# Layer-0 cross attention: weights normalised by token ahead of their transposes, outputs made feature by token, queries' bias on ScalarE

## The reference, cut to what matters

```python
g = jax.nn.relu(jnp.einsum('bnmd,hd->bhnm', emb, Wg) + bg[None, :, None, None])
q = (queries @ Wq.T + bq).reshape(b, nq, H, D_K).transpose(0, 2, 1, 3)
k = (keys @ Wk.T + bk).reshape(b, nk, H, D_K).transpose(0, 2, 1, 3)
v = (values @ Wv.T + bv).reshape(b, nk, H, D_V).transpose(0, 2, 1, 3)
a = jnp.einsum('bhqd,bhkd->bhqk', q, k) / jnp.sqrt(jnp.float32(D_K))
mn = jax.nn.softmax(jnp.log(jnp.clip(g, 1e-06, None)) + a, axis=-1)
out = jnp.einsum('bhqk,bhkd->bqhd', mn, v).reshape(b, nq, H * D_V)
return out @ Wo.T + bo
```

## Time and profile before

| what | value |
|---|---|
| median of three runs | 413.66 us (411.83 to 413.72) |
| the profiled execution, its own time | 412.39 us |
| its span in the trace | 410.6 us |
| mean granted TensorE clock | 0.91 of full speed |
| busy: TensorE, weight loads, DVE, ACT, GpSimd | 81%, 48%, 70%, 49%, 22% of the span |

### The profile page before, as it was taken

The page is one execution under the profiler, slowest core; times in us unless marked ns, Lnnn a source line. Parts: engine busy times, 40 slices in busy tenths (PEclk is TensorE's granted clock), DMA queues, the critical chain, the costliest instruction groups (busy, mean ns, idle before and its releaser), DMA issues.

```text
span 410.6 us, 8844 instructions
## 1 busy us (share of the span) xinstructions
PE 333.1 (81%) x3743; PEld 196.8 (48%) x3743; DVE 285.9 (70%) x420; ACT 201.5 (49%) x329; POOL 89.4 (22%) x85
## 2 busy tenths in 40 slices
PE   5277899999986999999998869647769986899721
PEld 1022333333322678889886634212247773577610
DVE  2779587888998666777766336898458746667475
ACT  2986976788986423222233435843424424243330
POOL 4101353455663270000000000000043412122000
PEclk9765899999999999999999999967989999699955
DMA  6920000023735500000000000000000000000001
GB/s 177 395 105 0 1 1 2 0 69 93 202 101 153 204 3 2 2 3 2 3 2 3 0 2 1 0 0 0 0 2 3 3 3 3 2 3 3 2 2 51
DMA packets 22137, 16.42 MB, mean 40 GB/s; under 512 B 17873, under 2 KB 19153, under 8 KB 21970
## 3 DMA queue, kind: packets, MB, share of 16 engines
q1 hardware_dynamic: 22098, 15.86, 12.1%
HBM read 11.13 MB, written 4.72 MB: 39 GB/s over the span
## 4 chain that ended last, share of the span: by engine, by line
PE 60%; DVE 18%; ACT 14%; issue 6%; DMA 1%; POOL 0%; DVEq 0%; SPq 0%; ACTq 0%; POOLq 0%
PE psum L441 52%; PE psum L754 3%; PE psum L623 2%; DVE small L1553 2%; PE psum L590 2%; ACT arena_b L996 1%; DVE arena_b L1415 1%; ACT psum L992 1%; DVE small L1629 1%; ACT arena_b L976 1%; ACT psum L987 1%; ACT logg L939 1%; ACT arena_b L982 1%; ACT arena_b L1134 1%; DVE arena_b L1599 1%
## 5 line engine op out<-in xcount | busy, mean ns | idle before, releaser
L441 PE MATMUL psum<-arena_b 64*64 64x9 f32 (+2 forms) x1316 | 46.2, 258 | 8.7 <-DVE arena_b L1633 5.5
L1227 POOL TENSOR_TENSOR arena_a<-arena_a,arena_b 128x1024 f32<-128x1024 f32 x15 | 31.8, 2121 | 62.2 <-DVE arena_b L1389 62.2
L441 PEld LDWEIGHTS psum<-arena_b 64*64 64x64 f32 (+2 forms) x1316 | 26.9, 137 | 22.8 <-issue 16.1
L1401 DVE TENSOR_TENSOR_SCAN arena_a<-arena_b,psum 128x512 f32<-128x512 f32 x32 | 37.4, 1206 | 0.4
L441 PE MATMUL psum<-arena_a,xw 128*128 128x128 f32 x256 | 33.5, 286 | 2.2 <-ACT arena_a L1041 2.2
L441 PE MATMUL psum<-arena_a 64*64 64x64 f32 (+2 forms) x1088 | 34.0, 245 | 0.3 <-DVE xn L1317 0.3
L441 PEld LDWEIGHTS psum<-arena_a,xw 128*128 128x128 f32 x256 | 31.2, 199 | 3.7 <-ACT arena_a L1041 2.7
L1629 DVE TENSOR_REDUCE small<-psum 128x16 f32<-128x1024 f32 x16 | 19.6, 1224 | 19.0 <-PE psum L441 19.0
L441 PEld LDWEIGHTS psum<-arena_a 64*64 64x64 f32 (+1 forms) x1088 | 21.8, 138 | 18.6 <-issue 9.6
L1262 POOL MEMSET arena_b<- 128x16 f32 x4 | 0.3, 128 | 139.3 <-DVE x L1619 139.3
L441 PE MATMUL psum<-xc,logg 128*128 128x512 f32 x32 | 21.3, 754 | 10.2 <-DVE sq L1375 10.2
(11 more groups left out here) (222 smaller groups left out, 671.6 us busy)
## 6 DMA issues: line engine op xcount, KB each, us to landing
g_scratch<-arena_a SPq DMA_DIRECT2D x64, 64.0 KB, 2.1
logg<-in_rkvo SPq DMA_DIRECT2D x8, 256.0 KB, 4.5
xw<-in_xw SPq DMA_DIRECT2D x1, 2048.0 KB, 10.7
logg<-g_scratch SPq DMA_DIRECT2D x2, 1024.0 KB, 5.1
logg<-g_scratch SPq DMA_DIRECT2D x1, 2048.0 KB, 7.8
ffn_w<-in_ffn SPq DMA_DIRECT2D x1, 576.0 KB, 11.3
x<-in_xT SPq DMA_DIRECT2D x2, 256.0 KB, 3.4
arena_a<-in_ctxT SPq DMA_DIRECT2D x1, 512.0 KB, 6.4
```

Source lines behind the costliest of these rows:

```text
L441: return nc.tensor.matmul(o, l, r, start=start, stop=stop, **kw)
L1227: g.tensor_tensor(two, two, pairs[n % 3][:, :, HALF + 1:], ALU.add).then_inc(s.ab_done, 1)
L1401: return v_.tensor_tensor_scan(sums[n % 3][:, i * HALF:(i + 1) * HALF], pairs[n % 3][:, i, 0:HALF], scan_mask, 0.0, ALU.add, ALU.mult)
```

## The change

Three things change in the cross attention, and with them the order on TensorE and ACT.

The softmax is finished before the transposes. The exponential is taken on the shifted scores in SBUF (ACT), then DVE sums them per token and head, takes the reciprocal and multiplies, and only then are the weights transposed; ACT copies the transposed weights. The values lose their column of ones, and GpSimd its four memsets.

The product is turned round. Values are now the stationary operand and weights the moving one, so that the outputs come as features by tokens, as the output projection wants them. The eight output transposes are gone, and ACT copies the outputs straight from pD.

The bias of the queries goes from two DVE operations to eight ACT operations with the bias as a column per partition. For the first tile they stand behind the second half of the layer norm on ACT.

TensorE's order for tile t is now: scores, keys t+1, product t-1, queries t+1, Wo t-1, values t+1, transposes t. The product's matmuls go over the sequence and the partition half within each pair of heads; before they went over both halves and then the next pair. Some semaphores are merged.

```diff
-OUT_HEADS = [4 * (i // 2) + 2 * par + i % 2
-             for par, i in [(0, i) for i in range(1, 8)] + [(1, i) for i in range(7)] + [(1, 7), (0, 0)]]
+OUT_HEADS = [4 * j + 2 * par + i for par in range(2) for j in range(4) for i in range(2)]
...
-            def x_out_transposed(t, u):
-                pe.wait_ge(s.on_done, t + 1)
-                for cc in range(NCH):
-                    last = nc.tensor.transpose(pB[:, cc * P:(cc + 1) * P], on_x[u][:, cc * P:(cc + 1) * P], ident)
-                last.then_inc(s.to_psum, 1)
+            def x_product(t, u):
+
+                pe.wait_ge(s.pt_done, t + 1)
+                pe.wait_ge(s.vx_done, 2 * t + 2)
+                if t:
+                    pe.wait_ge(s.x2_done, t)
+                for i in range(8):
+                    for b in range(2):
+                        for par in range(2):
+                            r = slice(64 * par, 64 * par + 64)
+                            at = P * (i // 2) + 64 * b
+                            last = mm(half(pD, par)[64 * (i % 2):64 * (i % 2) + 64, at:at + 64], v_x[u][b][r, i, :],
+                                      pt_x[u][r, 4 * (i % 2) + i // 2, 64 * b:64 * b + 64])
+                last.then_inc(s.o_psum, 1)
...
             def xattn(t, u, prev, nxt):
-                pe.wait_ge(s.q_done, 2 * t + 2)
+                pe.wait_ge(s.q_done, t + 1)
...
                 if prev:
-                    x_out_transposed(t - 1, 1 - u)
+                    x_product(t - 1, 1 - u)
+                pe.wait_ge(s.s_scaled, t + 1)
                 if nxt:
-                    pe.wait_ge(s.s_scaled, t + 1)
                     x_q(t + 1)
                 if prev:
                     x_wo(t - 1, 1 - u)
-                pe.wait_ge(s.s_done, t + 1)
-                if prev:
-                    pe.wait_ge(s.ot_done, t)
-                for cc in range(NCH):
-                    last = nc.tensor.transpose(pB[:, cc * P:(cc + 1) * P], s_x[u][:, cc * P:(cc + 1) * P], ident)
-                last.then_inc(s.t_psum, 1)
                 if nxt:
                     x_v(t + 1, 1 - u)
                 else:
...
-                pe.wait_ge(s.pt_done, t + 1)
-                pe.wait_ge(s.vx_done, 2 * t + 2)
+                pe.wait_ge(s.p_done, t + 1)
                 if prev:
-                    pe.wait_ge(s.x2_done, t)
-                for i in range(8):
-                    for par in range(2):
-                        for b in range(2):
-                            bank, at = o_place(par, i)
-                            r = slice(64 * par, 64 * par + 64)
-                            last = mm(bank[64 * b:64 * b + 64, at:at + 65],
-                                      pt_x[u][r, 4 * (i % 2) + i // 2, 64 * b:64 * b + 64], v_x[u][b][r, i, :])
-                last.then_inc(s.o_psum, 1)
+                    pe.wait_ge(s.pt_done, t)
+                for cc in range(NCH):
+                    last = nc.tensor.transpose(pB[:, cc * P:(cc + 1) * P], s_x[u][:, cc * P:(cc + 1) * P], ident)
+                last.then_inc(s.t_psum, 1)
...
-            x_out_transposed(TILES - 1, 1)
+            x_product(TILES - 1, 1)
             x_wo(TILES - 1, 1)
...
+            def x_queries(t, u):
+                act.wait_ge(s.q_psum, t + 1)
+                for cc in range(NCH):
+                    last = nc.scalar.activation(q_x[u][:, cc, :], pA[:, cc * P:(cc + 1) * P], ACT.Identity,
+                                                bias=p("xbq", cc))
+                last.then_inc(s.q_done, 1)
+
+            def x_exp(t, u):
+                act.wait_ge(s.s_done, t + 1)
+                nc.scalar.activation(s_x[u], s_x[u], ACT.Exp).then_inc(s.s_exp, 1)
+
+            def x_weights(t, u):
+                act.wait_ge(s.t_psum, t + 1)
+                nc.scalar.activation(pt_x[u].rearrange("p c t -> p (c t)"), pB[:, :], ACT.Copy).then_inc(s.pt_done, 1)
+
             def x_out(t, u):
-                act.wait_ge(s.to_psum, t + 1)
-                nc.scalar.activation(ot_x[u].rearrange("p c t -> p (c t)"), pB[:, :], ACT.Copy).then_inc(s.ot_done, 1)
+                act.wait_ge(s.o_psum, t + 1)
+                nc.scalar.activation(ot_x[u].rearrange("p c t -> p (c t)"), pD[:, :], ACT.Copy).then_inc(s.ot_done, 1)
 
             def xattn(t, u, prev, nxt):
                 if prev:
+                    x_weights(t - 1, 1 - u)
                     x_out(t - 1, 1 - u)
-                act.wait_ge(s.t_psum, t + 1)
-                nc.scalar.activation(pt_x[u].rearrange("p c t -> p (c t)"), pB[:, :], ACT.Exp).then_inc(s.pt_done, 1)
+                x_exp(t, u)
                 if nxt:
-                    if prev:
-                        act.wait_ge(s.o_psum, t)
+                    x_queries(t + 1, 1 - u)
                     x_values(t + 1, 1 - u)
...
             ln_rstd(1, 1)
-            act.wait_ge(s.v_ones, 4)
+            act.wait_ge(s.g_psum, 2 * BOX_STEPS)
+            x_queries(0, 0)
             x_values(0, 0)
...
             ln_square(2, 0)
+            x_weights(TILES - 1, 1)
             ln_rstd(2, 0)
...
             def xattn(t, u, prev, nxt):
-                if prev:
-                    x_norm(t - 1, 1 - u)
                 dve.wait_ge(s.s_psum, t + 1)
...
                 if nxt:
                     x_keys(t + 1, 1 - u)
-                if nxt:
-                    x_queries(t + 1, 1 - u)
+                total, inv = small[:, 64:80], small[:, 96:112]
+                dve.wait_ge(s.s_exp, t + 1)
+                v_.tensor_reduce(total, heads(s_x[u]), axis=AX.X, op=ALU.add).then_inc(s.s_sum, 1)
+                dve.wait_ge(s.s_sum, t + 1)
+                v_.reciprocal(inv, total).then_inc(s.s_inv, 1)
+                dve.wait_ge(s.s_inv, t + 1)
+                v_.tensor_tensor(heads(s_x[u]), heads(s_x[u]), cols(inv, S), ALU.mult).then_inc(s.p_done, 1)
                 if prev:
                     x_residual(t - 1)
...
-            x_queries(0, 0)
             ln_scale(1, 1)
```

More of the change, by code:

```diff
@@ L146, in build_program @@
         k_x = [ca(NCH * P).rearrange("p (c t) -> p c t", c=NCH) for _ in range(2)]
-        v_x = [[ca(8 * 65).rearrange("p (i d) -> p i d", i=8) for _ in range(2)] for _ in range(2)]
+        v_x = [[ca(8 * 64).rearrange("p (i d) -> p i d", i=8) for _ in range(2)] for _ in range(2)]
         q_x = [ca(NCH * P).rearrange("p (c t) -> p c t", c=NCH) for _ in range(2)]
@@ L150, in build_program @@
         pt_x = [ca(1024).rearrange("p (c t) -> p c t", c=NCH) for _ in range(2)]
-        on_x = [ca(1024) for _ in range(2)]
         ot_x = [ca(1024).rearrange("p (c t) -> p c t", c=NCH) for _ in range(2)]
@@ L273, in build_program @@
         s.o_psum = sem("o_psum")
-        s.o_inv = sem("o_inv")
-        s.on_done = sem("on_done")
-        s.to_psum = sem("to_psum")
+        s.s_exp = sem("s_exp")
+        s.s_sum = sem("s_sum")
+        s.s_inv = sem("s_inv")
+        s.p_done = sem("p_done")
         s.ot_done = sem("ot_done")
@@ L1239, in _ @@
                     r_y(n - 1)
-            pool.wait_ge(s.g_psum, 2 * BOX_STEPS)
-            for u in range(2):
-                for b in range(2):
-                    g.memset(v_x[u][b][:, :, 64:65], 1.0).then_inc(s.v_ones, 1)
             w3 = ffn_w[:].rearrange("p (k i) -> p k i", i=BLK)
@@ L1250, in _ @@
             pool.wait_ge(s.w_s, 1)
-            g.tensor_tensor(t3, w3, cols(wq_r, BLK), ALU.mult).then_inc(s.w_n, 1)
-            pool.wait_ge(s.w_n, 1)
-            g.tensor_scalar(wq_t, wq_t, MAGIC, MAGIC, ALU.add, ALU.subtract).then_inc(s.w_r, 1)
-            pool.wait_ge(s.w_r, 1)
-            g.tensor_scalar(wq_t, wq_t, 7.0, -8.0, ALU.min, ALU.max).then_inc(s.w_c, 1)
-            pool.wait_ge(s.w_c, 1)
+            g.tensor_tensor(t3, w3, cols(wq_r, BLK), ALU.mult).then_inc(s.w_step, 1)
+            pool.wait_ge(s.w_step, 1)
+            g.tensor_scalar(wq_t, wq_t, MAGIC, MAGIC, ALU.add, ALU.subtract).then_inc(s.w_step, 1)
+            pool.wait_ge(s.w_step, 2)
+            g.tensor_scalar(wq_t, wq_t, 7.0, -8.0, ALU.min, ALU.max).then_inc(s.w_step, 1)
+            pool.wait_ge(s.w_step, 3)
             g.tensor_tensor(t3, t3, cols(wq_s, BLK), ALU.mult).then_inc(s.w_q, 1)
@@ L1466, in _ @@
             residual1(1)
-            def x_queries(t, u):
-                dve.wait_ge(s.q_psum, t + 1)
-                for k in range(2):
-                    v_.tensor_tensor(q_x[u][:, 4 * k:4 * k + 4, :], half(pA, k).rearrange("p (c t) -> p c t", c=4),
-                                     cols(p("xbq")[:, 4 * k:4 * k + 4], P), ALU.add).then_inc(s.q_done, 1)
             def x_keys(t, u):
@@ L1478, in x_keys @@
                     .then_inc(s.kx_done, 1)
-            def x_norm(t, u):
-                dve.wait_ge(s.o_psum, t + 1)
-                inv = small[:, 64:80]
-                banks = [bank[:, :].rearrange("p (k c) -> p k c", k=2)[:, :, 0:65 * n]
-                         .rearrange("p k (h d) -> p k h d", d=65) for bank, n in ((pD, 7), (pB, 1))]
```

(12 more changed lines are left out.)

10 lines of the change are left out of this document (2 added, 8 removed).

## The result

The changed kernel takes 417.19 us (median of five runs, four of them at 416.85 to 418.32) against 413.67 us before: ratio 1.0088, 95% interval 1.0052 to 1.0123. It is slower by 0.9%, about 3.6 us. The forecast was 412.8 us with a range up to 416.5, so the time lies outside the range, and on the other side of the old one. One run of the change (645.16 us), one of e3 (540.19, the only one traced there) and one of e4 (575.05) were disturbed executions, far outside all the others, and no range or ratio here counts them. The profiled execution took 417.17 us (span 415.4), the one before 412.39 (span 410.6).

What follows compares the result with a forecast made beforehand. TensorE's own work was taken to bound the steady tiles of the layer-0 cross attention. Terms +1.45 + 1.05 - 2.6 - 0.8 = -0.9 us gave a median of 412.8 us, range 409.3 to 416.5 (the forecast's own 411 to 414.5).

Steps and rivals of the forecast that it cites:

- E0: End of tile 0's scores on TensorE, where the key projection's slot starts; 144.64 us in the kernel before.
- E1: The same mark one tile later, end of tile 1's scores; 153.69 us in the kernel before.
- E7: The same mark for tile 7, six steady periods after tile 1's; 220.89 us in the kernel before.
- start: Start of the cross attention: first scores wait for ACT's eight queries operations, at 145.0 instead of 143.55; +1.45 us.
- tile 0: First tile, softmax chain bare without a previous tile's work; 10.1 us between scores' ends instead of 9.05, +1.05 us.
- six tiles: Steady tiles, bound by TensorE: output transposes gone, three more tile-size changes; period 10.76 instead of 11.20, -2.6 us.
- tail: From tile 7's scores to the layer norm's second mean: about 15.5 us instead of 16.97; half counted, -0.8 us.
- Rival A: Steady tiles: added tile-size changes nearly free, period 10.33 to 10.43, net -2.9 to -4.2 us; chance 0.28.
- Rival B: Product's new order halves its concurrency: 1.9 us instead of 1.0, period 11.7, net +5.8 us; chance 0.08.
- Rival C: TensorE idling at start and tile 0 brings a 1.2 GHz stretch costing 1.7 us, no tail gain: +1.6; chance 0.14.
- Rival D: Loop through DVE and ACT bounds the steady tile if mispriced by 0.7 us; 6 us per microsecond beyond; chance 0.05.

Runs made afterwards that it cites:

- e3: The changed kernel with the product's 32 matmuls ordered so that neighbours go to different 64x64 quarters of the array; 416.53 us, ratio 1.0084 against the kernel before.
- e4: The changed kernel with the product directly behind the scores, ahead of the keys, and ACT's copy of the values moved with it; 414.40 us, ratio 1.0023.
- e1: The changed kernel with GpSimd's last product of the feed-forward weights held until DVE's subtraction of tile 0 is done; 414.64 us, ratio 1.003.
- e5: The kernel before with seven small dependent DVE operations ahead of the last normalisation, to hold the first scores back; 419.99 us, ratio 1.0164.
- e2: The changed kernel with the bias of tile 0's queries back on DVE, the other tiles' still on ACT; 411.08 us, ratio 0.9954.
- e6: The changed kernel with tile 0's query bias on DVE, quarters order, product behind scores, GpSimd's last product behind tile 0's multiplication; 409.64 us, ratio 0.9924.

## Why the prediction was wrong

By its own steps, with E0, E1 and E7 as it defined them, and the old tail of the second trace before:

```
step            forecast  measured  how
start           +1.45     +1.49     15.74 - 14.25
tile 0          +1.05     +2.92     11.97 - 9.05; two of four traces 0.4 and 0.7 more
six tiles       -2.6      -1.95     65.23 - 67.18
tail            -0.8       0.0      15.37 - 15.34
sum             -0.9      +2.5      +2.8 with the mean of the four traces
```

**The start** was right: the first scores are released by the last of ACT's eight queries operations, which took 2.15 us against 2.26 forecast. The 0.26 us from there to the first matmul was not in the forecast; the two small errors, and a start 0.09 us ahead of the exponential's end, nearly cancel.

**Tile 0 is the step that failed**, 1.9 us of the miss. The step reads "from E: scaling at 0.24, maximum 1.49, subtraction 2.74 to 3.97" and takes DVE's durations from a steady tile. There GpSimd is idle; in tile 0 it is not. The prediction said of GpSimd only that it "loses four memsets off the path"; it never laid GpSimd's rows beside DVE's new times. The trace of the kernel before already had the answer, in rows that I had not read:

```profile
147.40 1.23 DVE L1517 TENSOR_TENSOR arena_a<-arena_a,small 128x1024 f32<-128x1024 f32 x1
```

```profile
147.54 2.09 POOL L1255 TENSOR_SCALAR arena_b<-arena_b 128x1152 f32<-128x1152 f32 x1
149.72 2.13 POOL L1257 TENSOR_TENSOR arena_b<-arena_b 128x1152 f32<-128x1152 f32 x1
```

Before, the subtraction started 0.14 us ahead of a GpSimd operation, and it was GpSimd that paid: 2.09 us instead of 1.15 (e1). The product followed at 149.72, when the next DVE operations had at most one operand in SBUF. Measured from GpSimd's first row of this work (140.82 before, 141.80 after), DVE's chain is 1.5 us later in the changed kernel and the product 0.95 us sooner, since the operation ahead of it isn't lengthened any more. So the subtraction starts 0.12 us behind the product.

The Trainium skill ("SBUF — State Buffer", section "SBUF: two separate sides") states this as a rule: a DVE operation with two SBUF inputs and a GpSimd operation that reads SBUF take a shared pair of ports as an exclusive lock for the whole instruction, and the one that starts second blocks fully. The runs here agree for the products: blocked fully the subtraction would take 151.88 - 149.87 + 1.22 = 3.23 us and took 3.09, and operations with one SBUF input went on at 1.22. In e5 the normalisation's 3.25 is 0.54 less than the same sum gives (147.24 - 144.18 + 0.73 = 3.79), so there it wasn't blocked for its whole length. It was a rule that spoke against this change, and I had not weighed it.

That e1 then hits the forecast's 10.1 us is in part luck: the forecast put the exponential at 4.15 us behind E0, behind a copy of the previous outputs that tile 0 doesn't have. In e1 it started at 4.09, 0.11 us after the subtraction's end, a hand-off that the forecast had left out.

**The steady tiles** had the right mechanism and the wrong size: 0.33 us a tile instead of 0.44. Rival A (changes of tile size free) fell: three of the slots that leave full size are 1.98, 1.98 and 1.03 against 1.78, 1.79 and 0.87 where full size follows. Of the forecast 10.76 the transposes were 0.05 too dear, while the product's slot was 1.14, not 1.02, and the scores' 1.09, not 1.02. I had put the loads' duration alone there and left out the 0.07 for leaving 64x64 that I had read myself, twice; the other 0.05 is the order of the quarters. Rival B (two tiles at a time, 1.9 us) fell with the product's 1.14; its price was also added up too high (10.76 + 0.88 = 11.64 gives a steady loss of 2.6 us, not 3.1). Over six tiles the slots' difference is 0.65 us of the miss.

**The tail** was a wrong reading, 0.8 us of the miss. The new one came out at 15.37 against 15.5 forecast. The old one, 16.97, was a single execution's clock; the second trace has 15.34, and the third the same tail within 0.01 us. I saw the low clock in the earlier trace rows and still counted half of the difference as a gain.

**Rival C** (clock) was right in its place and too dear in its price: 0, 0.41 and 0.66 us in tile 0, not 1.7. **Rival D** had a mispriced DVE chain as its mechanism, but in the steady tiles, where nothing came of it; the chain closed with 0.74 us to spare (its last product ends at 188.85, the transposes start at 189.59), and in tile 0, which has none, I had taken it as certain.

**What stays open.** The steps give +2.8 us, the ratios +3.6 (2.2 to 5.1) and +4.1 (2.7 to 5.5). The traced times (means 412.92 and 416.28, +3.4) are accounted for: +2.2 in the stage (with the first trace's long old tail), +0.15 ahead of it, +0.5 in the feed-forward, +0.5 in layer 1, in code that the change does not touch. But these parts scatter by 1.3 and 2.7 us over the traces in the table of pieces, so three and four traces don't say whether that last microsecond belongs to the change.

The mean granted clock of each execution, which is on record also for those without a trace, points at a part of it. It was 0.894 to 0.899 in ten executions of the change (medians 417.19 and 417.53 us). In the 31 of the kernel before that stood beside e1 it was 0.894 to 0.913; eight of these had 0.899 or less and took 415.0 us on average, against a median of 413.85 for all. The two of the kernel before at 0.899 or less beside the second group of the change, on the same chip, took 415.34 and 415.59. At like clock the change is thus some 2.0 to 2.6 us slower, near the steps' sum, and the rest goes with the clock. e2 and e6 have 0.908 on average and are 1.4 and 1.6 us faster than their stage's pieces say, though still within their intervals. Whether the late start of the scores lowers the clock in later code, or the two only go together, no run shows.

## What to carry to other kernels

When an edit moves or adds an operation outside the steady loop, lay the timeline of every engine over its new place, GpSimd's above all, and look for pairs of operations that lengthen each other; a duration from a steady tile doesn't hold where GpSimd works in SBUF beside it. Price each group's slot from start to start of the next group, not by its loads. Where a stretch shows a clock below 1.00, take a second trace before counting it as a gain.

## What the runs showed of the hardware

- DVE operations with two operands in SBUF and GpSimd operations lengthen each other: the subtraction 1.23 to 3.09 and 2.07, the multiplication 1.22 to 1.55, the normalisation 0.73 to 3.25; in the other direction GpSimd's TENSOR_SCALAR 1.15 to 2.09. The second operand may be small: the subtraction's is 128x16, read again and again.
- Beside the same GpSimd product, DVE's addition with an operand in PSUM and its reduction kept 1.22 us (e1).
- The one that starts second pays, and 0.12 to 0.15 us decide it: GpSimd at 149.75 and DVE at 149.87 in the changed kernel, DVE at 148.21 and GpSimd at 148.36 in e2.
- Leaving full tile size costs 0.16 to 0.21 us; a 64x64 group of 64 loads has a slot of 1.09 us, or 1.14 in the order in which neighbours share a half of the output partitions.
- The same program gets its low-clock stretches at different places: 17.50 and 15.85 us for the same tail, 11.88 to 12.54 for the same tile 0.
